# Drives of three states made by ScalarE with time on the partitions, one buffer for the rows of B: a Mamba recurrence on one core

## The chip, the core and the metric

The kernel runs on 1 core of one Trainium2 chip. The time is the device time of one execution in microseconds (us). Lower is better.

## The reference, cut to what matters

The input is x of shape (4, 64, 32, 32). A Mamba block works on two channel orders of each of the 4 images, so on 8 sequences of 1024 steps with 128 inner channels and 16 states. Attention and a chain of small attention and feed-forward steps follow. The change touches the recurrence alone:

```
xc = conv(xi);  u = silu(xc + conv_b)
x_dbl = u @ W_x.T;  dt = softplus(x_dbl[..., :4] @ W_dt.T + b_dt)
Bs, Cs = x_dbl[..., 4:20], x_dbl[..., 20:]
A = -exp(A_log)
# for each step t, channel d, state n:
h[d, n] = exp(dt[t, d] * A[d, n]) * h[d, n] + (dt[t, d] * u[t, d]) * Bs[t, n]
y[t, d] = sum_n h[d, n] * Cs[t, n]
out = ((y + u * D_skip) * silu(z)) @ W_out.T
```

## The kernel before, in words

**Units.** The recurrence is cut into 128 units: `u = 16 * q + n` is state n of sequence q, `NS` is 16. All tiles of a unit have the 128 channels on the partitions and the 1024 time steps along the row. A unit has four parts. The decay `exp(dt * A)` is one ScalarE instruction (`act_exp`, L1324). The drive is `dtu * B`, where `dtu` is dt times u and B's row n is the same on all partitions. The scan (`dve_unit`, L1641) is one VectorE instruction over 1024 steps. The product of the scan's result with C's row (`pool_hc`, L1956) is GpSimd's, and TensorE adds these products of 16 states up in PSUM (`pe_sum`, L816, with the identity as weights, `LAG` = 3 units behind).

**Who makes the drive.** For 10 of 16 states, here called own units, TensorE spreads B's row over the partitions into the PSUM tile `pb[u % 2]` with a selector matrix (`pe_b`, L804, bf16), VectorE multiplies it by `dtu` in place (L1636), and the decay lies in one of three SBUF buffers `da`. For the other six (`POOLED` = 1, 4, 7, 9, 12, 14), a DMA spreads B's row from DRAM scratch into `bb[k % 2]` (`sp_b`, L2127), GpSimd multiplies by `dtu` into `dbu[k % 2]` (`pool_drive`, L1967), and the decay goes into the free `pb[u % 2]`, so that its `act_exp` waits for scan u - 2.

**Order.** Every engine has its own hand-written loop over u. An engine does its instructions in order and waits at semaphores. Beside the units the loops prepare sequence q + 1 at fixed states n:

```
TensorE  n=0: pe_x   n=1: pe_gate(q)  n=3: pe_bc   n=4,6: pe_bc_less  n=7: pe_dt  n=9,10: pe_dt_add
ScalarE  n=1: act_x  n=2: act_gate(q) n=4: act_hi  n=5: act_mid  n=6: act_lo
         n=8,9: act_dt, act_one, act_ln      n=11,12: act_dt_out
VectorE  n=3: dve_y(q-1)                     n=11,12: dve_dtu
```

In iteration u, TensorE does `pe_b(u + 1)` and then `pe_sum(u - 3)`. ScalarE does `act_exp(u + 1)` first, but in iteration n = 1 it does both `act_exp(u + 1)` and `act_exp(u + 2)` ahead of `act_x`, and none at n = 2. GpSimd does `pool_drive(u + 2)` and then `pool_hc(u)`. SyncE does `sp_c(u)`, C's row, and then `sp_b(u + 3)`.

**Three dependences that matter.** `act_x` (SiLU, in another table set, so behind an ACT_TABLE_LOAD) gives u of sequence q + 1. `pe_gate(q)` waits for it, since both use the bank `px[h]`. The sum of state 15 of sequence q - 1 (`pe_sum` at n = 2) stands behind `pe_gate` on TensorE, and `dve_y` at n = 3 waits for that sum. In even sequences `pe_out_late` (L845, n = 14) stands ahead of the next sequence's first `pe_b`.

The two loops around these, as far as they matter here:

```
if u == 0 or n != AHEAD + 1:
    act_exp(act, u + 1)
if n == AHEAD:
    act_exp(act, u + 2)
for h in range(2):
    if q < LAST:
        if n == 1:
            act_x(act, q + 1, h)
```

## Time and profile before

| what | value |
|---|---|
| median of 3 runs | 709.54 us (708.71 to 710.75) |
| the profiled execution, own time | 711.64 us |
| its span, from the first to the last instruction | 709.8 us |
| mean granted TensorE clock | 0.961 |
| first to last scan of the recurrence | 33.2 to 443.7 us of the span |

The profile shows one execution. "Busy" is the time that an engine spent in instructions, idle time is counted before an instruction with the engine or DMA that ended it, and PEld is TensorE's weight load, which runs beside its matmuls. Times in the timeline are from the start of the span.

### The profile page before, as it was taken

The page shows a single profiled execution, that of the slowest core. Times are in us where ns is not written, and L with a number is a line of the kernel's source. Part 1 is how long each engine was busy: PE and PEld are TensorE (multiplying, and loading weights), DVE is VectorE, ACT ScalarE, POOL GpSimd, SP SyncE. Part 2 cuts the span into 40 slices and gives each one's busy share as a digit, 9 for nine tenths or more (in the row PEclk, how much of TensorE's full clock was granted, in tenths as well). Part 3 has the DMA queues.
Part 4 walks back from the last instruction along what each step waited for, and adds up shares of the span by engine and source line. Part 5 has one row for each costly group of instructions (what it writes and reads, how often), then busy time and mean ns, then how long its engine had stood idle before and what let it go on. Part 6 is the DMA issues. An engine that isn't in the chain of part 4 may idle for free.

```text
span 709.8 us, 10911 instructions
## 1 busy us (share of the span) xinstructions
PE 618.5 (87%) x3732; PEld 267.0 (38%) x3732; DVE 581.7 (82%) x622; ACT 415.2 (59%) x643; POOL 451.1 (64%) x240
## 2 busy tenths in 40 slices
PE   8889879889877888988878887988979999999996
PEld 3323222222222212222222222345756446777771
DVE  5799999999999999999999999364365457788755
ACT  4878777668567566766774663353445525544441
POOL 7599999999999999999999999510000220000002
...
GB/s 104 220 267 211 230 227 291 226 259 226 232 232 253 211 250 211 236 217 210 234 233 222 234 241 115 1 1 0 3 5 8 1 20 1 1 2 1 2 2 65
DMA packets 32107, 101.20 MB, mean 143 GB/s; under 512 B 6821, under 2 KB 7342, under 8 KB 32046
## 3 DMA queue, kind: packets, MB, share of 16 engines
...
q10 hardware_dynamic: 1240, 0.88, 0.4%
...
q14 instruction: 28, 0.23, 0.1%
...
## 4 chain that ended last, share of the span: by engine, by line
PE 44%; DVE 23%; issue 19%; ACT 7%; POOL 5%; DMA 1%; DVEq 0%; ACTq 0%; POOLq 0%
DVE hh_all L1641 9%; DVE pb L1636 8%; PE py L279 7%; PE pb L242 6%; PE px L302 5%; PE py L816 5%; POOL hc L1956 4%; PE pb L1044 2%; PE py L1068 2%; PE px L845 2%; PE pb L804 2%; POOL dbu L1967 2%; PE px L292 1%; DVE dtu_all L1615 1%; PE px L763 1%
## 5 line engine op out<-in xcount | busy, mean ns | idle before, releaser
L1956 POOL TENSOR_TENSOR hc<-hh_all,cc 128x1024 f32<-128x1024 f32 x128 | 298.5, 2355 | 6.3 <-DVE hh_all L1641 4.6
L1641 DVE TENSOR_TENSOR_SCAN hh_all<-da,pb 128x1024 f32<-128x1024 f32 x80 | 182.9, 2286 | 3.4 <-ACT da L1324 0.4
L1970 POOL TENSOR_TENSOR yg<-w_xs 128x512 f32<-128x512 f32 x10 | 12.6, 1266 | 227.1 <-DVE w_xs L1783 132.7
L816 PE MATMUL py<-hc,w_cst 64*64 64x512 f32 x1024 | 148.2, 639 | 8.5 <-DVE yg L1652 8.5
L1967 POOL TENSOR_TENSOR dbu<-bb,dtu_all 128x1024 f32<-128x1024 f32 x48 | 113.2, 2358 | 5.0 <-DMA bb<-scr 5.0
L1641 DVE TENSOR_TENSOR_SCAN hh_all<-pb,dbu 128x1024 f32<-128x1024 f32 x48 | 108.9, 2269 | 2.0 <-DVE dtu_all L1615 1.7
L1636 DVE TENSOR_TENSOR pb<-pb,dtu_all 128x1024 f32<-128x1024 f32 x80 | 97.1, 1214 | 3.7 <-PE pb L804 1.2
L804 PE MATMUL pb<-bc,w_sel 128*128 128x512 bf16 x160 | 51.8, 408 | 53.1 <-DVE hh_all L1641 53.0
L1324 ACT ACTIVATE da<-dt_all,w_aneg 128x1024 f32<-128x1024 f32 x80 | 89.8, 1138 | 2.7 <-DVE dt_all L1622 1.8
L1324 ACT ACTIVATE pb<-dt_all,w_aneg 128x1024 f32<-128x1024 f32 x48 | 53.6, 1116 | 64.3 <-DVE hh_all L1641 63.8
L816 PEld LDWEIGHTS py<-hc,w_cst 64*64 64x64 f32 x1024 | 31.2, 136 | 80.9 <-issue 54.4
L804 PEld LDWEIGHTS pb<-bc,w_sel 128*128 128x128 bf16 x160 | 11.0, 99 | 113.4 <-DVE hh_all L1641 83.8
L335 DVE TENSOR_REDUCE gate_all<-pb 128x1 f32<-128x128 f32 (+7 forms) x32 | 22.8, 752 | 19.6 <-PE pb L252 19.5
L279 PE MATMUL py<-w_cst,dbu 128*128 128x128 f32 x208 | 30.3, 286 | 8.1 <-ACT dbu L402 4.8
L402 ACT ACTIVATE bb<-pb,gate_all 128x1024 f32<-128x1024 f32 (+4 forms) x32 | 28.6, 898 | 7.8 <-DVE gate_all L335 7.8
L402 ACT ACTIVATE dbu<-pb,gate_all 128x1024 f32<-128x1024 f32 (+3 forms) x32 | 30.3, 952 | 4.8 <-DVE gate_all L335 4.8
L242 PE MATMUL pb<-w_xs,u_all 64*128 64x512 f32 x128 | 31.8, 615 | 0.0
L410 ACT ACTIVATE da<-py 128x512 f32<-128x512 f32 (+2 forms) x20 | 9.8, 510 | 37.3 <-PE py L279 37.1
L410 ACT ACTIVATE cc<-py 128x512 f32<-128x512 f32 (+1 forms) x20 | 10.7, 553 | 34.6 <-PE py L279 34.6
L355 DVE COPY da<-py 128x512 f32<-128x512 f32 (+2 forms) x28 | 16.1, 610 | 17.6 <-PE py L279 17.6
L279 PE MATMUL py<-w_cst,bb 128*128 128x128 f32 x192 | 27.2, 279 | 3.8 <-ACT bb L402 3.8
L279 PEld LDWEIGHTS py<-w_cst,dbu 128*128 128x128 f32 x208 | 23.2, 144 | 19.1 <-issue 12.4
...
## 6 DMA issues: line engine op xcount, KB each, us to landing
cc<-scr SPq DMA_DIRECT2D x128, 512.0 KB, 4.3
...
```

Of the source, the lines that this page charges most:

```text
L242: part = nc.tensor.matmul(self.s[r][:, o + a:o + a + m], self.qt[rows, g * 128:(g + 1) * 128], self.kt[rows, p * L + a:p * L + a + m], sta ...
L279: last = nc.tensor.transpose(self.pt[:, o + j:o + j + 128], self.p[g % 2][r][:, j:j + 128], self.w["cst"][:, IDN:IDN + 128])
L302: last = nc.tensor.matmul(bank[C * r:C * r + C, 0:128], self.vv[:, p * 8 + j, r, :], self.pts[g % 2][r][:, j * 128:(j + 1) * 128], start=( ...
L335: self.nc.vector.tensor_reduce(self.nm[:, i:i + 1], self.s[r][:, self.start(g):self.start(g) + 128 * self.blocks(g)], AX.X, ALU.max, negat ...
L402: self.nc.scalar.activation(self.p[g % 2][r][:, 0:n], self.s[r][:, self.start(g):self.start(g) + n], ACT.Exp, bias=self.nm[:, i:i + 1], ac ...
L804: last = nc.tensor.matmul(pb[u % 2][:, half(h)], w["sel"][:, n, :], bc3[q % 2][:, half(h)], start=True, stop=True)
L816: last = nc.tensor.matmul(py[part(t), half(r)], ident[part(r), part(r)], hc[u % NHC][part(r), half(t)], start=(n == 0), stop=(n == NS - 1) ...
L1324: nc.scalar.activation(to[:, :], dt[q % 2][:, :], ACT.Exp, scale=w["aneg"][:, n:n + 1]).then_inc(da_done, 1)
L1636: nc.vector.tensor_tensor(pb[u % 2][:, :], pb[u % 2][:, :], dtu[q % 2][:, :], ALU.mult).then_inc(dbu_done, 1)
L1641: nc.vector.tensor_tensor_scan(hh[u % NHH][:, :], decay[:, :], drive[:, :], 0.0, ALU.mult, ALU.add).then_inc(scan_done, 1)
L1956: nc.gpsimd.tensor_tensor(hc[u % NHC][:, :], hh[u % NHH][:, :], cc[u % NCC][:, :], ALU.mult).then_inc(hc_done, 1)
L1967: nc.gpsimd.tensor_tensor(dbu[k % NDB][:, :], bb[k % 2][:, :], dtu[q % 2][:, :], ALU.mult).then_inc(pooled_done, 1)
```

## The change

In sequences 2, 4 and 6 (`FLIPS`) the states are dealt out anew. GpSimd makes the drives of five states (3, 6, 8, 11, 13). States 1, 5 and 15 (`FLIPPED`) are made by ScalarE: with time on the partitions, B of one state is one number per partition, so a drive is eight activations of 128x128 with a scale taken from a column of `b_t` (`act_flip_drive`). Eight TensorE transposes bring it back into `pb` (`pe_b`), and VectorE scans it with no product of its own. The other eight states are own units as before. For this, TensorE transposes B's rows (`pe_flip_b`, n = 7 of the sequence before) and `dtu` (`pe_flip_dtu`, n = 13), and ScalarE copies both to SBUF (`act_flip_b`, `act_flip_dtu`). `pe_dt` of half 1 moves from n = 7 to n = 8 there. The transposed `dtu` lies in `bb[1]`, so the rows of B have `bb[0]` alone in all sequences: `sp_b` waits until GpSimd has made the drive before, and is issued one unit later (u + 2). The two tiles of ScalarE's drives are `ex` and `rl`, which the softplus of the next sequence uses too. `pe_late` moves by one unit.

```diff
-        POOLED = (1, 4, 7, 9, 12, 14)
-        NP = len(POOLED)
+        FLIPS = (2, 4, 6)
+        POOLED = [(3, 6, 8, 11, 13) if q in FLIPS else (1, 4, 7, 9, 12, 14) for q in range(NSEQ)]
+        FLIPPED = [(1, 5, 15) if q in FLIPS else () for q in range(NSEQ)]
...
+        dtu_t, drive_t = bb[1], [ex, rl]
+        b_t = sb("b_t", [128, 128])
...
+        def pe_flip_b(pe, s):
+            pe.wait_ge(px_free[1], freed(s, 1) + 1)
+            pe.wait_ge(bcf_done, 2 * s + 2)
+            for j in range(L // 128):
+                last = nc.tensor.transpose(px[1][:, NS * j:NS * j + NS], bcf[0:NS, j * 128:j * 128 + 128], cst[0:NS, IDN:IDN + NS])
+            last.then_inc(px_full[1], 1)
...
         def pe_b(pe, u):
...
+            if flipped(u):
+                t = flip_count(u)
+                pe.wait_ge(flip_drive, t + 1)
+                for j in range(0, L, 128):
+                    last = nc.tensor.transpose(pb[u % 2][:, j:j + 128], drive_t[t % 2][:, j:j + 128], ident)
+                last.then_inc(b_full, 1)
+                return
...
                         if n == 7:
+                            if h and q + 1 in FLIPS:
+                                pe_flip_b(pe, q + 1)
+                            else:
+                                pe_dt(pe, q + 1, h)
+                        if n == 8 and h and q + 1 in FLIPS:
                             pe_dt(pe, q + 1, h)
+                        if n == 13 and q + 1 in FLIPS:
+                            pe_flip_dtu(pe, q + 1, h)
...
+        def act_flip_b(act, s):
+            act.wait_ge(px_full[1], full(s, BT, 1))
+            atleast(act, flip_drive, flip_count(NS * (s - 1)))
+            nc.scalar.activation(b_t[:, :], px[1][:, 0:128], ACT.Copy).then_inc(flip_in, 1)
...
+        def act_flip_drive(act, u):
...
+            for j in range(L // 128):
+                last = nc.scalar.activation(drive_t[t % 2][:, j * 128:j * 128 + 128], dtu_t[:, j * 128:j * 128 + 128], ACT.Identity,
+                                            scale=b_t[:, NS * j + n:NS * j + n + 1])
+            last.then_inc(flip_drive, 1)
...
+                if n == 7 and q + 1 in FLIPS:
+                    act_flip_b(act, q + 1)
+                act_flip_drive(act, u + 2)
+                if n == 13 and q + 1 in FLIPS:
+                    for h in range(2):
+                        act_flip_dtu(act, q + 1, h)
...
-                nc.vector.tensor_tensor(pb[u % 2][:, :], pb[u % 2][:, :], dtu[q % 2][:, :], ALU.mult).then_inc(dbu_done, 1)
-                dve.wait_ge(dbu_done, k + 1)
+                if not flipped(u):
+                    nc.vector.tensor_tensor(pb[u % 2][:, :], pb[u % 2][:, :], dtu[q % 2][:, :], ALU.mult).then_inc(dbu_done, 1)
+                    dve.wait_ge(dbu_done, product_count(u) + 1)
...
-            atleast(sp, pooled_done, k - 1)
-            sp.dma_start(bb[k % 2][:, :], scr[q % 2, n:n + 1, :].broadcast_to((128, L))).then_inc(bb_in[k % 2], 16)
+            atleast(sp, pooled_done, k)
+            sp.dma_start(bb[0][:, :], scr[q % 2, n:n + 1, :].broadcast_to((128, L))).then_inc(bb_in, 16)
```

**What moves on ScalarE at the start of sequence 2.** From the weight copy that ends sequence 1 (`w_bp`) to the decay of state 4. `da` and `pb` are where a decay goes, `u_all<-px` is `act_x`, `gate_all<-px` is `act_gate`. Before:

```order
L1283 ACTIVATE w_bp<-px,w_vcol 128x1
L1324 ACTIVATE pb<-dt_all,w_aneg 128x1024
L1324 ACTIVATE da<-dt_all,w_aneg 128x1024 x2
L1235 ACT_TABLE_LOAD
L1235 ACTIVATE u_all<-px,w_vcol 128x512 x2
L1305 ACTIVATE gate_all<-px 128x512 x2
L1521 ACT_TABLE_LOAD
```

In the change:

```order
L1336 ACTIVATE w_bp<-px,w_vcol 128x1
L1407 ACTIVATE da<-dt_all,w_aneg 128x1024 x2
L1407 ACTIVATE pb<-dt_all,w_aneg 128x1024
L1285 ACT_TABLE_LOAD
L1285 ACTIVATE u_all<-px,w_vcol 128x512 x2
L1388 ACTIVATE gate_all<-px 128x512 x2
L1610 ACT_TABLE_LOAD
```

The decay into `pb` was that of state 1 and stood first of the three. It is now that of state 3 and stands last of the three, straight ahead of the table load and `act_x`.

**What moves on TensorE in sequence 1, states 7 and 8.** `px<-u_all` is `pe_dt`, one row for each half, and `py<-hc` is `pe_sum`. Before:

```order
L804 MATMUL pb<-bc_1,w_sel 128x512 x2
L816 MATMUL py<-hc,w_cst 64x512 x4
L763 MATMUL px<-u_all,w_wts 128x512 x2
L816 MATMUL py<-hc,w_cst 64x512 x4
```

In the change:

```order
L847 MATMUL pb<-bc_1,w_sel 128x512 x2
L859 MATMUL py<-hc,w_cst 64x512 x4
L785 MATMUL px<-u_all,w_wts 128x512
L792 MATMUL px<-w_cst,bcf 128x16 x8
L859 MATMUL py<-hc,w_cst 64x512 x4
L785 MATMUL px<-u_all,w_wts 128x512
```

The transposes of B (L792) stand behind `pe_dt` of half 0.

**What moves on ScalarE at the same place.** From `act_lo` (`bc_0<-px 32x512`) to the first half's softplus. Before:

```order
L1250 ACTIVATE bc_0<-px 32x512 x2
L1324 ACTIVATE da<-dt_all,w_aneg 128x1024
L1324 ACTIVATE pb<-dt_all,w_aneg 128x1024
L1256 ACTIVATE ex<-px,w_vcol 128x512
```

In the change:

```order
L1300 ACTIVATE bc_0<-px 32x512 x2
L1407 ACTIVATE da<-dt_all,w_aneg 128x1024
L1354 ACTIVATE b_t<-px 128x128
L1407 ACTIVATE pb<-dt_all,w_aneg 128x1024
L1309 ACTIVATE ex<-px,w_vcol 128x512
```

The copy of the transposed B stands between the decays of states 8 and 9, ahead of the softplus.

## Rows read from the trace of the kernel before

**Rows 1.** The page: busy us (share of the span) and instructions of each engine

```profile
PE 618.5 (87%) x3732; PEld 267.0 (38%) x3732; DVE 581.7 (82%) x622; ACT 415.2 (59%) x643; POOL 451.1 (64%) x240
```

**Rows 2.** Windows, mid recurrence: length, busy PE, PEld, DVE, ACT, POOL, clock, DMA, GB/s

```profile
160.00:210.00 50.00, 42.55 (x227) 12.53 (x225) 48.68 (x30) 34.48 (x44) 50.00 (x23) 1.00 0.66 232
```

**Rows 3.** The page's costliest groups: busy us, mean ns | idle before, releaser

```profile
L1956 POOL TENSOR_TENSOR hc<-hh_all,cc 128x1024 f32<-128x1024 f32 x128 | 298.5, 2355 | 6.3 <-DVE hh_all L1641 4.6
L1967 POOL TENSOR_TENSOR dbu<-bb,dtu_all 128x1024 f32<-128x1024 f32 x48 | 113.2, 2358 | 5.0 <-DMA bb<-scr 5.0
L1636 DVE TENSOR_TENSOR pb<-pb,dtu_all 128x1024 f32<-128x1024 f32 x80 | 97.1, 1214 | 3.7 <-PE pb L804 1.2
```

**Rows 4.** Waits of VectorE, 55 to 445 us: total us, times, longest

```profile
DVE pb L1636 <- PE pb L804: 1.2, 2, 0.9
```

**Rows 5.** Timeline, VectorE, sequence 1, states 9 to 11: start us, us

```profile
112.39 2.26 DVE L1641 TENSOR_TENSOR_SCAN hh_all<-pb,dbu 128x1024 f32<-128x1024 f32 x1
...
115.81 2.29 DVE L1641 TENSOR_TENSOR_SCAN hh_all<-da,pb 128x1024 f32<-128x1024 f32 x1
...
119.25 2.29 DVE L1641 TENSOR_TENSOR_SCAN hh_all<-da,pb 128x1024 f32<-128x1024 f32 x1
```

**Rows 6.** Timeline, ScalarE, sequence 1: decay 9, softplus, decay 11

```profile
109.06 1.12 ACT L1324 ACTIVATE pb<-dt_all,w_aneg 128x1024 f32<-128x1024 f32 x1 [1.92 <-DVE hh_all L1641]
110.21 0.69 ACT L1256 ACTIVATE ex<-px,w_vcol 128x512 f32<-128x512 f32 x1
110.79 0.68 ACT L1257 ACTIVATE rl<-px,w_vcol 128x512 f32<-128x512 f32 x1
...
117.59 1.14 ACT L1324 ACTIVATE da<-dt_all,w_aneg 128x1024 f32<-128x1024 f32 x1
```

**Rows 7.** Timeline, TensorE, sequence 1, state 7

```profile
106.90 0.61 PE L804 MATMUL pb<-bc,w_sel 128*128 128x512 bf16 x2 [2.20 <-DVE hh_all L1641]
...
108.46 1.98 PE L763 MATMUL px<-u_all,w_wts 128*128 128x512 f32 x4
```

**Rows 8.** The page: groups of 128x128 transposes in the attention, with their weight loads

```profile
L279 PE MATMUL py<-w_cst,dbu 128*128 128x128 f32 x208 | 30.3, 286 | 8.1 <-ACT dbu L402 4.8
...
L279 PEld LDWEIGHTS py<-w_cst,dbu 128*128 128x128 f32 x208 | 23.2, 144 | 19.1 <-issue 12.4
```

**Rows 9.** Timeline, ScalarE, start of sequence 4

```profile
239.87 1.28 ACT L1235 ACT_TABLE_LOAD   x1
241.16 1.26 ACT L1235 ACTIVATE u_all<-px,w_vcol 128x512 f32<-128x512 f32 x2
...
245.69 1.12 ACT L1324 ACTIVATE pb<-dt_all,w_aneg 128x1024 f32<-128x1024 f32 x1 [0.19 <-DVE hh_all L1641]
```

**Rows 10.** Timeline, TensorE, start of sequence 4: gate, B of state 3, sum 15

```profile
241.90 1.65 PE L793 MATMUL px<-w_xs,w_wts 64*64 64x512 f32 x8 [0.17 <-ACT u_all L1235]
243.49 0.61 PE L804 MATMUL pb<-bc,w_sel 128*128 128x512 bf16 x2
244.02 1.09 PE L816 MATMUL py<-hc,w_cst 64*64 64x512 f32 x8
```

**Rows 11.** Timeline, VectorE, start of sequence 4: the two halves of y

```profile
245.57 1.26 DVE L1652 TENSOR_TENSOR yg<-py,gate_all 128x512 f32<-128x512 f32 x2
```

**Rows 12.** Timeline, TensorE and VectorE, end of sequence 4

```profile
281.84 0.61 PE L804 MATMUL pb<-bc,w_sel 128*128 128x512 bf16 x2 [1.62 <-DVE hh_all L1641]
...
286.83 0.60 PE L804 MATMUL pb<-bc,w_sel 128*128 128x512 bf16 x2
...
287.54 1.23 DVE L1636 TENSOR_TENSOR pb<-pb,dtu_all 128x1024 f32<-128x1024 f32 x1
```

**Rows 13.** Landings of `bb` (60 to 440 us), then one of `cc` at 191 us; GpSimd's timeline

```profile
DMA to landing us min/median/max: 4.6/5.0/7.8
...
DMA to landing us min/median/max: 3.4/3.4/3.4
...
207.12 4.65 POOL L1956 TENSOR_TENSOR hc<-hh_all,cc 128x1024 f32<-128x1024 f32 x2
```

More of the change, by code:

```diff
@@ L502, in pooled, with flipped, flip_count, product_count @@
         def pooled(u):
-            return u % NS in POOLED
+            return u % NS in POOLED[u // NS]
+        def flipped(u):
+            return u % NS in FLIPPED[u // NS]
         def pool_count(u):
-            return NP * (u // NS) + sum(1 for n in POOLED if n < u % NS)
+            return sum(1 for v in range(u) if pooled(v))
+        def flip_count(u):
+            return sum(1 for v in range(u) if flipped(v))
+        def product_count(u):
+            return own_count(u) - flip_count(u)
         def own_count(u):
@@ L764, in pe_dt, with pe_flip_dtu @@
                              skip_group_check=True).then_inc(px_full[h], 1)
+        def pe_flip_b(pe, s):
[4 more added lines that the diff above has]
+            last.then_inc(px_full[1], 1)
+        def pe_flip_dtu(pe, s, h):
+            pe.wait_ge(px_free[h], freed(s, h) + 2 + h)
+            pe.wait_ge(dtu_done, 2 * s + h + 1)
+            for j in range(0, HALF, 128):
+                last = nc.tensor.transpose(px[h][:, j:j + 128], dtu[s % 2][:, h * HALF + j:h * HALF + j + 128], ident)
+            last.then_inc(px_full[h], 1)
         def pe_dt_add(pe, s, h):
@@ L1230, in act_x @@
         def act_x(act, s, h):
-            act.wait_ge(px_full[h], full(s, X))
+            act.wait_ge(px_full[h], full(s, X, h))
             if s >= 2:
@@ L1254, in act_dt @@
         def act_dt(act, s, h):
-            act.wait_ge(px_full[h], full(s, DT))
+            act.wait_ge(px_full[h], full(s, DT, h))
+            if s - 1 in FLIPS:
+                used = max(n for n in FLIPPED[s - 1] if n < 9)
+                act.wait_ge(b_full, own_count(NS * (s - 1) + used) + 1)
             nc.scalar.activation(ex[:, half(h)], px[h][:, :], ACT.Abs, bias=w["bdt"][:, :])
@@ L2153, in _ @@
             sp_scratch(sp, 0)
-            for u in range(3):
+            for u in range(2):
                 sp_b(sp, u)
```

101 lines of the change are left out of this document (63 added, 38 removed).

## The prediction

> **What bounds the kernel now.** I read the page's busy line first [rows 1]: no engine is full over the whole span, so it decides nothing, and the stage must be looked at by itself. The windows of the recurrence do that [rows 2]: in 50 us GpSimd is busy for 50.0, VectorE for 48.7, and ScalarE for 34.5. Two engines are full there. The groups give their work [rows 3]: GpSimd has 22 products of 2.36 us a sequence, some 51 us (a little less, since neighbours overlap), and VectorE has 16 scans, ten products of 1.21 us and small work, also some 51 us. The waits say that neither has slack: VectorE waits for its products' input only twice, 1.2 us in all [rows 4], and GpSimd waits 4.6 us for scans in the whole recurrence [rows 3]. So a microsecond comes off only if it comes off both, and a wait on either costs its full length. That is how each edit is priced: on VectorE's path, with GpSimd's looked at for what it supplies.
>
> **What is removed.** In each of sequences 2, 4 and 6 VectorE makes 8 products where it made 10. A product takes 1.21 us [rows 3], with the step to the next instruction 1.23. From scan to scan with a product it is 119.25 - 115.81 = 3.44 [rows 5], so 2.21 without. Two in three sequences: 6 x 1.23 = **-7.4**. GpSimd has one product less in each, 3 x 2.32 = 7.0 (half of the 4.65 for two [rows 13]). Both full engines get about the same relief, so it could all count, and this is the most that the change can bring. What ScalarE and TensorE are given lies beside that, unless one of their results is late. I went through each for what stands behind it.
>
> **Preparing B, sequences 1, 3 and 5.** ScalarE's copy of transposed B stands ahead of the decay of state 9. TensorE can start on it only when it has done B's row of state 8 (106.90, released by scan 6), a sum, and `pe_dt` of half 0, which starts at 108.46 and takes half of 1.98 [rows 7], so at 109.45. Eight transposes of 16 rows are not in the trace; full ones are, at 23.2 / 208 = 0.11 us for each weight load [rows 8], so I take 0.9, which gives 110.35, and 0.15 for the copy. ScalarE starts decay 9 at 110.5 and not at 109.06 [rows 6]: **1.45 later**. From there to decay 11 it works without a gap: softplus from 110.21, decay 11 from 117.59 to 118.73 [rows 6]. VectorE starts scan 11 at 119.25 [rows 5], so it has 0.5 to spare. It waits 1.45 - 0.5 = 0.95. Three times: **+2.9**. Bounds: nothing, if ScalarE's copy comes 1 us earlier than I think, and 2 us each, where TensorE is granted the lower clock at that moment. The shift of `pe_dt` of half 1 costs nothing: it is needed 4 us after decay 9.
>
> **The start of sequences 2, 4 and 6.** This is the place I trust least and that weighs most. The decay of state 3 goes into `pb`, waits for scan 1, and stands directly ahead of the table load and `act_x`. Before, these three decays were done before scan 1 had ended, and the load came at 239.87 [rows 9]. Now the chain runs from the end of scan 1: the decay 1.12 and 0.05 to start (the latter an estimate), the load 0.02 + 1.29 (239.87 to 241.16), the gate's matmuls 0.74 after the first SiLU started, 1.6 for them (241.90 to 243.49), and the first half of the sum of state 15, 0.55 of 1.09 [rows 9, 10]. That is 5.4 us to the first half of y. VectorE in the same time does the product and scan of state 2, 1.23 + 2.2 = 3.45, and then wants y. Before, the sum ended at 245.1 and y started at 245.57 [rows 10, 11], straight behind the scan. So each of the three now waits 5.4 - 3.45 = 1.9: **+5.7**. Lower end 1.3 each, the gate at its shortest; upper end 2.4, if the sum's second half is what y waits for.
>
> At this load a page speaks against the change. The row shows a load that starts as the decay ends and is over in 1.29 us, with the SiLU right behind it [rows 9]; my chain goes by that. The Trainium skill (ScalarE: Activation LUTs, What ACT_TABLE_LOAD costs) gives 1283 ns for the load and some 1380 ns for a drain at each switch. It is a rival below.
>
> The transposes of the first flipped drive also stand ahead of `pe_x` on TensorE, and they wait for scan 15 of the sequence before. They make the product of state 2 up to 0.8 late. That lies inside the wait for y and costs nothing as long as that wait is there.
>
> **ScalarE's drives.** Eight activations of 128 columns with a scale from SBUF. Two of 512 columns with such an operand start 0.58 apart; between 0.69 for 512 and 1.14 for 1024 a column costs 0.88 ns, so for 128 I take 0.58 - 0.34 = 0.24, and with the last one's end 2.1 us for a drive [rows 6]. The ends are 1.2, half of it, and 3. State 1's is made in the idle end of the sequence before, and state 15's behind decay 14 with some 3 us to spare. State 5's falls behind decay 4. By the chain above it and decay 5 are done 1 us before scan 5 wants them, because VectorE has waited for y. Nothing for the three.
>
> **The end of sequences 2, 4 and 6.** TensorE goes from scan 13 to B's row of the next sequence without a gap: 281.84 to 287.43, and VectorE's product starts at 287.54, right behind [rows 12]. Eight transposes at 30.3 / 208 = 0.146 [rows 8] take 1.2 to 1.3 in place of 0.6: 0.65 later, less the 0.1 of slack. **+0.5** each, 1.5 in all. The ends are 0 and 1.5 each (at 0.27 a transpose, the duration of a lone one).
>
> **One buffer for B.** A row is now fetched only when GpSimd's drive before it is done. Where pooled states are 2 apart (two such pairs a sequence, 16 in all), two products of C, 4.65 us, lie between. `bb` landed after 4.6 to 7.8, median 5.0, but it always followed a `cc` by 0.4 us; a transfer of the same size with nothing ahead landed after 3.4 [rows 13]. Now C's row of that unit was issued two products earlier and B's row goes first. I take 4 us, so it is hidden under those products; in some it will not be: **+0.3**. The ends are 0 and 16 x 0.45 = 7. Behind this wait on SyncE's queue C's next row is held by one GpSimd product, 2.3 us; it is wanted four such products later.
>
> **The sum.** -7.4 + 2.9 + 5.7 + 1.5 + 0.3 = **+3.0 us**. For the profiled execution that is 711.64 + 3.0 = 714.6. That execution was 2.1 above the median of the runs, which is what I forecast: 709.54 + 3.0 = 712.5 us.
>
> **Rivals.**
> - *The waits for y do not come, and the relief arrives.* The place is state 3 of sequences 2, 4, 6; the point is whether the chain from scan 1 to y is under 3.5 us. For it: ScalarE has 15 of 50 us free [rows 2], and the relief is equal on both full engines. Against it: each link of the chain is a row. -7.4 + 2.9 + 1.5 + 0.3 = -2.7: 706.8. If the preparation is hidden too, 704. Chance 0.18.
> - *The wait for y stands and the two others are hidden*, as the order of the two small waits depends on tenths of a microsecond: -7.4 + 5.7 + 0.3 + 1 = -0.4: 709.1. Chance 0.22.
> - *The single buffer is late.* If B's row lands after 5.0 as before, every near pair costs 0.4: +6.4, part of it inside other waits, so 3.0 + 4 = 7: 716.5. For it: the median. Against it: the order on the queue. Chance 0.12.
> - *The switch of tables waits for ScalarE to run empty when it follows directly on a decay.* The place is the load behind the decay of state 3. If that costs as long as the load itself again, 1.29 [rows 9], the chain to y grows by so much in three sequences: 3.0 + 3.9 = 6.9: 716.4. No wait stands behind the load in the row, so 0.05. By the figure of the page named above this would be 3 x 1.38 = 4.1 instead, an estimate.
>
> **How the numbers follow.** About 0.3%, 2.1 us, is what a measurement of this kernel can tell from no change: under 707.4 is faster, over 711.7 slower. The forecast itself has 0.43, nearly all above 711.7. Slower gets 0.58, with the third and fourth rival; within 0.3%, 0.23, which is the second rival and the edge of the forecast; faster 0.19. The range goes from the first rival to beyond the third: 706.5 to 717.5. The bounds of the terms alone would reach from 705 to over 720.
>
> **What would show it.** Right: in sequences 2, 4 and 6 VectorE sits idle for some 2 us ahead of y, released by TensorE's sum (L859) or shows it as a wait for `py`; a wait of about 1 us at scan 11 of sequences 1, 3 and 5, released by ScalarE's decay; 0.5 at the first product of sequences 3, 5 and 7, released by TensorE. GpSimd waits for `bb` under 1 us in all. Wrong: if VectorE has no wait at y, the second largest term is gone and the kernel is faster. If GpSimd waits for `bb` at most near pairs, the buffer term was too small. If the flipped scans (states 1, 5, 15) wait for `pb`, I had ScalarE's drives or their transposes too short.

## The result and the profile after

| | before | the change |
|---|---|---|
| median in one job (4 runs each) | 710.14 us | 721.77 us (719.73 to 724.35) |
| ratio | | 1.0181, 95% interval 1.0155 to 1.0206 |
| profiled execution, own time | 711.64 us | 721.56 us |
| its span, mean granted TensorE clock | 709.8 us, 0.961 | 719.8 us, 0.962 |
| end of the last scan of the recurrence | 443.7 us | 458.1 us |

The change is slower by 1.8%, some 12 to 13 us, where 3 were forecast. In the profiled execution the recurrence ends 14.4 us later. What follows it, code that the change does not touch, took 261.7 us there and 266.1 before. In a later run it took 260.2, so that part scatters between executions, and I compare by sequence below.

First the page of the change: busy time of the engines, then the groups that answer to [rows 3].

```profile
PE 627.3 (87%) x3840; PEld 276.7 (38%) x3840; DVE 575.6 (80%) x616; ACT 440.1 (61%) x724; POOL 445.5 (62%) x237
...
L2046 POOL TENSOR_TENSOR hc<-hh_all,cc 128x1024 f32<-128x1024 f32 x128 | 299.6, 2359 | 24.1 <-PE py L859 12.7
L2057 POOL TENSOR_TENSOR dbu<-bb,dtu_all 128x1024 f32<-128x1024 f32 x45 | 106.1, 2358 | 7.3 <-DMA bb<-scr 7.3
...
L1726 DVE TENSOR_TENSOR pb<-pb,dtu_all 128x1024 f32<-128x1024 f32 x74 | 89.9, 1215 | 12.7 <-PE pb L847 10.5
```

These are lines of the whole page; `py` is TensorE's sum, `hc` GpSimd's product with C. The work went as announced: 74 products on VectorE, 45 drives on GpSimd. But GpSimd idles 24.1 us ahead of its products of C, 12.7 of them for TensorE's sums. VectorE's waits in the recurrence (33 to 456 us; total, times, longest) are the view that answers to [rows 4]:

```profile
DVE pb L1726 <- PE pb L847: 10.5, 9, 4.3
DVE hh_all L1731 <- POOL dbu L2057: 4.9, 5, 3.4
DVE hh_all L1731 <- ACT pb L1407: 2.4, 4, 1.0
...
DVE hh_all L1731 <- ACT da L1407: 1.9, 5, 0.4
DVE yg L1742 <- PE py L859: 1.8, 2, 1.0
```

The wait for y, my largest cost, is 1.8 in all. Ten microseconds go to B's rows from TensorE and five to GpSimd's drives. I had nothing of that size for either. To see where, take the start of the first scan of each sequence from the timeline and subtract it from the next one's (us):

| sequence | 0 | 1 | 2 | 3 | 4 | 5 | 6 |
|---|---|---|---|---|---|---|---|
| before | 52.0 | 50.5 | 51.1 | 50.9 | 51.1 | 52.4 | 50.7 |
| the change | 52.1 | 55.1 | 56.0 | 53.4 | 51.7 | 53.5 | 51.7 |
| forecast difference | 0 | +0.95 | -0.1 | +0.95 | -0.1 | +0.95 | -0.1 |
| measured difference | 0 | +4.6 | +4.9 | +2.5 | +0.6 | +1.1 | +1.0 |

(The forecast for sequences 2, 4 and 6 is -2.46 + 1.9 + 0.5; the 0.3 for the buffer is spread over all.) Two thirds of the loss lie in sequences 1 and 2. How much such a value scatters is shown by sequence 0, where only the buffer of B differs: over all profiles of this study it took 51.5 to 53.7. A difference of 1 in one profile means little. Sequence 2 moves more than that with TensorE's clock (below), so a wait with its releaser says more than a length.

**Sequence 1: SyncE's queue.** Timeline of SyncE's issues before (first fence) and in the change (second): `w_xs<-w_xm` are the spreads of the inputs of sequences 4, 5 and 6, each a pair of transfers of 256 KB, of which the first is shown.

```profile
100.66 0.47 SPq L2148 DMA_DIRECT2D w_xs<-w_xm  x1
...
104.15 0.47 SPq L2148 DMA_DIRECT2D w_xs<-w_xm  x1
...
108.06 0.43 SPq L2127 DMA_DIRECT2D bb<-scr  x1
108.61 0.47 SPq L2148 DMA_DIRECT2D w_xs<-w_xm  x1
```

```profile
105.27 0.32 SPq L2216 DMA_DIRECT2D bb<-scr  x1
105.68 0.47 SPq L2237 DMA_DIRECT2D w_xs<-w_xm  x1
...
109.16 0.47 SPq L2237 DMA_DIRECT2D w_xs<-w_xm  x1
...
111.20 1.45 SPq L2237 DMA_DIRECT2D w_xs<-w_xm  x1
...
114.38 0.81 SPq L2216 DMA_DIRECT2D bb<-scr  x1
```

With one buffer the `bb` of 105.27 had to wait for GpSimd's drive before it. The three pairs of spreads stood behind it, so they started 5.0, 5.0 and 2.6 us later and closer together, ahead of the `bb` of state 12, which was issued at 114.38 and not at 108.06. The four `cc` issued between 110 and 118 us landed after 9.1 to 10.0 us (the median over the kernel is 4.5), that of 110.32 at 119.38. Then, on GpSimd and VectorE:

```profile
119.50 2.36 POOL L2046 TENSOR_TENSOR hc<-hh_all,cc 128x1024 f32<-128x1024 f32 x1 [2.38 <-issue]
...
120.14 2.29 DVE L1731 TENSOR_TENSOR_SCAN hh_all<-da,pb 128x1024 f32<-128x1024 f32 x1 [0.41 <-ACT da L1407]
...
124.02 2.35 POOL L2057 TENSOR_TENSOR dbu<-bb,dtu_all 128x1024 f32<-128x1024 f32 x1 [2.15 <-DMA bb<-scr]
...
126.40 2.29 DVE L1731 TENSOR_TENSOR_SCAN hh_all<-pb,dbu 128x1024 f32<-128x1024 f32 x1 [3.40 <-POOL dbu L2057]
```

GpSimd stops for 2.38 us, until that row of C has landed, and for 2.15 until the row of B has, and scan 12 waits 3.40. Scan 11 starts at 120.14 against 119.25 [rows 5], so the preparation of B costs 0.89 here; I had said 0.95.

**The start of sequence 2: a chain of three engines.** Timeline of TensorE, ScalarE and VectorE in the change:

```profile
135.91 0.87 PE L963 MATMUL px<-w_cst,w_xs 128*128 128x128 f32 x5
136.60 0.28 ACT L1328 ACTIVATE w_xs<-px 128x128 f32<-128x128 f32 x1 [2.65 <-PE px L963]
...
138.88 2.44 ACT L1377 ACTIVATE ex<-bb,b_t 128x128 f32<-128x128 f32 x8
...
141.47 1.06 PE L843 MATMUL pb<-w_cst,ex 128*128 128x128 f32 x8 [2.71 <-ACT ex L1377]
...
143.91 2.07 PE L754 MATMUL px<-w_xs,w_wts 128*128 128x512 f32 x2
...
148.67 0.59 PE L847 MATMUL pb<-bc,w_sel 128*128 128x512 bf16 x2
...
149.31 1.23 DVE L1726 TENSOR_TENSOR pb<-pb,dtu_all 128x1024 f32<-128x1024 f32 x1 [4.25 <-PE pb L847]
```

The late weights are turned (L963), ScalarE copies them and a decay, makes the first flipped drive until 141.32, TensorE transposes it, and only then comes `pe_x` with B's row of state 2 behind it. The product of state 2 waits 4.25 us. The first two pairs of `pe_x` took 2.07 and 1.34 us where later ones take 1.02, which is TensorE at the lower of its two clocks (1.2 GHz against 2.4) for part of the way: the granted clock was 0.65 in 132 to 138 us and, behind the idle 2.71 us of the row at 141.47, 0.80 in 144 to 150. At the end of the sequence the clock fell again: the first product of sequence 3 waited 2.41 us for its row of B. These waits account for the length: 51.1 before, less 2.46 for the two products, plus 4.25, 2.41, 0.50 for a drive of GpSimd and 0.24 for a decay, is 56.0.

### The profile page after: what moved, and what is told of

Read it like the earlier page. It is cut to its first block, busy times and chain, and to the rows that moved or that the text cites. A ratio compares the mean times of both kernels' runs of the same rounds, so it can differ in the third digit from the quotient of the medians.

```text
span 719.8 us, 11232 instructions
## 1 busy us (share of the span) xinstructions
PE 627.3 (87%) x3840; PEld 276.7 (38%) x3840; DVE 575.6 (80%) x616; ACT 440.1 (61%) x724; POOL 445.5 (62%) x237
## 4 chain that ended last, share of the span: by engine, by line
PE 46%; DVE 19%; issue 15%; ACT 13%; POOL 3%; DMA 2%; DVEq 0%; SPq 0%; ACTq 0%; POOLq 0%
DVE hh_all L1731 8%; PE py L279 7%; PE pb L242 6%; PE py L859 5%; PE px L302 5%; DVE pb L1726 5%; ACT da L1407 2%; PE pb L1087 2%; POOL hc L2046 2%; PE py L1111 2%; PE px L888 2%; PE pb L847 2%; POOL dbu L2057 1%; PE px L292 1%; PE px L754 1%
## 5 line engine op out<-in xcount | busy, mean ns | idle before, releaser
L2046 POOL TENSOR_TENSOR hc<-hh_all,cc 128x1024 f32<-128x1024 f32 x128 | 299.6, 2359 | 24.1 <-PE py L859 12.7
L1731 DVE TENSOR_TENSOR_SCAN hh_all<-da,pb 128x1024 f32<-128x1024 f32 x83 | 188.9, 2284 | 6.1 <-DVE pb L1726 1.9
L859 PE MATMUL py<-hc,w_cst 64*64 64x512 f32 x1024 | 152.0, 649 | 9.7 <-DVE yg L1742 6.1
L2060 POOL TENSOR_TENSOR yg<-w_xs 128x512 f32<-128x512 f32 x10 | 12.7, 1270 | 222.4 <-DVE w_xs L1873 132.7
L2057 POOL TENSOR_TENSOR dbu<-bb,dtu_all 128x1024 f32<-128x1024 f32 x45 | 106.1, 2358 | 7.3 <-DMA bb<-scr 7.3
L1731 DVE TENSOR_TENSOR_SCAN hh_all<-pb,dbu 128x1024 f32<-128x1024 f32 x45 | 102.4, 2276 | 8.9 <-POOL dbu L2057 4.9
L1726 DVE TENSOR_TENSOR pb<-pb,dtu_all 128x1024 f32<-128x1024 f32 x74 | 89.9, 1215 | 12.7 <-PE pb L847 10.5
L1407 ACT ACTIVATE da<-dt_all,w_aneg 128x1024 f32<-128x1024 f32 x83 | 93.6, 1141 | 6.5 <-DVE hh_all L1731 3.6
L847 PE MATMUL pb<-bc,w_sel 128*128 128x512 bf16 x148 | 47.6, 405 | 41.0 <-DVE hh_all L1731 40.9
L1407 ACT ACTIVATE pb<-dt_all,w_aneg 128x1024 f32<-128x1024 f32 x45 | 50.1, 1114 | 43.2 <-DVE hh_all L1731 42.0
```

What stands on the lines that cost most here:

```text
L847: last = nc.tensor.matmul(pb[u % 2][:, half(h)], w["sel"][:, n, :], bc3[q % 2][:, half(h)], start=True, stop=True)
L859: last = nc.tensor.matmul(py[part(t), half(r)], ident[part(r), part(r)], hc[u % NHC][part(r), half(t)], start=(n == 0), stop=(n == NS - 1) ...
L1407: nc.scalar.activation(to[:, :], dt[q % 2][:, :], ACT.Exp, scale=w["aneg"][:, n:n + 1]).then_inc(da_done, 1)
L1726: nc.vector.tensor_tensor(pb[u % 2][:, :], pb[u % 2][:, :], dtu[q % 2][:, :], ALU.mult).then_inc(dbu_done, 1)
L1731: nc.vector.tensor_tensor_scan(hh[u % NHH][:, :], decay[:, :], drive[:, :], 0.0, ALU.mult, ALU.add).then_inc(scan_done, 1)
L2046: nc.gpsimd.tensor_tensor(hc[u % NHC][:, :], hh[u % NHH][:, :], cc[u % NCC][:, :], ALU.mult).then_inc(hc_done, 1)
```

## The experiments

All times of a sequence are read as above, from one profile each. "The change" below is the kernel after. The kernel before was run in each job (medians 709.3, 708.2, 709.4 and 709.9 us) and the ratios are to it; they are not exactly the quotients of the medians. e7_spread and all runs from e10_best on have the spreads apart.

| run | median us | ratio, 95% interval | seq. 1 | 2 | 3 | 4 | 5 | 6 |
|---|---|---|---|---|---|---|---|---|
| e1_single | 713.95 | 1.0066 (1.0038 to 1.0095) | 54.8 | 51.6 | 52.4 | 50.8 | 50.9 | 50.8 |
| e2_slots | 720.33 | 1.0149 (1.0104 to 1.0194) | 53.1 | 55.1 | 53.6 | 53.3 | 53.3 | 51.7 |
| e3_late | 724.6 | 1.0217 (1.0147 to 1.0287) | 53.4 | 52.4 | 53.6 | 51.7 | 53.8 | 51.7 |
| e4_swap | 722.58 | 1.0177 (1.0130 to 1.0224) | 53.6 | 54.2 | 53.6 | 52.8 | 53.5 | 53.3 |
| e7_spread | 721.52 | 1.0128 (1.0047 to 1.0208) | 52.9 | 51.8 | 53.5 | 51.7 | 53.5 | 53.3 |
| e8_two | 720.48 | 1.0136 (1.0077 to 1.0196) | 54.0 | 51.6 | 54.6 | 53.4 | 53.5 | 51.7 |
| e9_xfirst | 724.28 | 1.0255 (1.0171 to 1.0338) | 55.6 | 56.6 | 53.5 | 51.9 | 53.5 | 52.1 |
| e10_best | 716.8 | 1.0107 (1.0080 to 1.0134) | 51.1 | 52.2 | 54.6 | 53.5 | 53.5 | 52.0 |
| e11_endb | 715.51 | 1.0087 (1.0052 to 1.0122) | 51.7 | 53.1 | 51.5 | 51.7 | 51.3 | 53.4 |
| e12_one3 | 719.2 | 1.0106 (1.0055 to 1.0157) | 53.1 | 54.8 | 53.5 | 52.7 | 53.5 | 52.8 |
| e13_all2 | 709.5 | 0.9993 (0.9974 to 1.0013) | 50.9 | 51.4 | 52.5 | 52.8 | 51.4 | 51.1 |
| e14_all3 | 712.69 | 1.0024 (0.9996 to 1.0052) | 51.0 | 53.5 | 51.5 | 51.1 | 51.5 | 51.1 |
| e15_sum2 | 707.8 | 0.9969 (0.9946 to 0.9993) | 50.5 | 51.1 | 50.9 | 49.7 | 51.5 | 51.3 |
| e16_sum3 | 707.15 | 0.9955 (0.9926 to 0.9984) | 50.5 | 50.4 | 51.5 | 50.2 | 51.4 | 51.4 |

### The single buffer alone, and two buffers where they fit

```diff
-        FLIPS = (2, 4, 6)
+        FLIPS = ()
```

> The change without flipped sequences: the deal of states of the kernel before in all sequences, but one buffer for the rows of B, fetched two units ahead. Queue theory: SyncE waits for the buffer ahead of the spreads of xs in sequence 1, the next row of B then lands late behind them; GpSimd and VectorE lose 4 to 5 us in sequence 1 and under 1 us in all other sequences together: 714 to 716 us. Near-pair theory (the row always comes too late where two pooled states are 2 apart): 0.4 us at each of 16 pairs, in every sequence: 716 to 718 us, and sequence 1 no worse than the others. If neither buffer cost is real: 710 us.

The run also keeps the later issue of B's rows (u + 2) and `pe_late` one unit later. 1.0066, and +4.3 us in sequence 1. Sequence 3 is 1.5 longer, 5 is 1.5 shorter, the others of the table within 0.5. VectorE's waits:

```profile
DVE hh_all L1731 <- POOL dbu L2057: 3.9, 2, 3.5
```

Both waits, 3.5 and 0.35 us, are in sequence 1; the near pairs of the other sequences show none. The queue theory holds and the near-pair theory falls.

```diff
-            sp.dma_start(bb[0][:, :], ...
+            sp.dma_start(bb[slot(u)][:, :], ...
```

(`slot(u)` alternates between both buffers outside the flipped sequences and is 0 inside; the row is then issued at u + 3 again, and ScalarE's copy of the transposed `dtu` waits for one drive of GpSimd more.)

> The change with two buffers for the rows of B wherever the second does not hold the transposed dtu (sequences 0, 1, 3, 5, 7, the last pooled state of each in the first buffer), fetched three units ahead there. Queue theory: sequence 1 falls from 55.1 to some 51.5 us, nothing else changes: 721.8 - 3.5 = 718 us. If the 55.1 come from the copy of B on ScalarE instead: under 1 us is gained.

The waits for GpSimd's drives and for `bb` in sequence 1 are gone, but it falls by 2.0 and no more. The preparation of B, 0.89 in the change, now makes VectorE wait 0.94, 0.83, 0.28 and 0.41 us. TensorE's clock made the difference:

```profile
107.82 1.01 PE L853 MATMUL pb<-bc,w_sel 128*128 128x512 bf16 x2 [3.01 <-DVE hh_all L1738]
```

The same row of B took 0.60 us in the change, after 2.19 us of idle, and the granted clock in 108 to 112 us was 0.59 here and 1.00 there. Sequence 2 hardly changed, and the whole came out 1.4 us under the change and not 3.5.

### The turn of B elsewhere

```diff
-                if n == 7 and q + 1 in FLIPS:
+                if n == 8 and q + 1 in FLIPS:
                     act_flip_b(act, q + 1)
```

> The change with ScalarE's copy of the transposed B behind the softplus of half 0 (state 8) and not ahead of the decay of state 9. Theory of the copy's wait: the waits of VectorE at states 9 to 11 of sequences 1, 3 and 5 go (0.9, 2.5 and 2.5 us in the trace): 721.8 - 5 = 717 us, less in sequence 1, where the buffer's wait lies behind it. Rival, the lower TensorE clock at state 8 alone makes them late: 721 us.

The decay was free, but the bank of `px` was not: `pe_dt` of half 1 waits for the copy to have read it, and B's row of state 10 stands behind that on TensorE. Sequence 3, timeline of e3_late:

```profile
222.37 1.10 PE L785 MATMUL px<-u_all,w_wts 128*128 128x512 f32 x2 [2.06 <-ACTq L1356]
...
223.94 1.23 DVE L1726 TENSOR_TENSOR pb<-pb,dtu_all 128x1024 f32<-128x1024 f32 x1 [1.52 <-PE pb L847]
```

The expectation failed: sequences 3 and 5 stayed at 53.6 and 53.8, with a wait for TensorE in place of one for ScalarE. So later (with the spreads apart, as in e7_spread below) both were moved to state 13, behind the last use of that bank:

```diff
-                if n == 7 and q + 1 in FLIPS:
-                    act_flip_b(act, q + 1)
                 act_flip_drive(act, u + 2)
                 if n == 13 and q + 1 in FLIPS:
+                    act_flip_b(act, q + 1)
```

(and `pe_flip_b` at n = 13 ahead of `pe_flip_dtu`, with the order of pieces to match)

> With the spreads of xs apart (as in the run before), B's rows are turned and copied at state 13 of the sequence ahead, just ahead of the turned dtu, and no longer at state 7 ahead of decay 9. My theory: the turn of B costs about 2.4 us of a sequence where it stands now, because ScalarE's decays 9 to 11 stand behind the copy, which waits for TensorE; at state 13 ScalarE has time. Sequences 1, 3 and 5 fall to 51.5, 51.5 and 52.4 (52.9, 53.5 and 53.5 with the spreads apart alone), the others as there (51.7, 51.7, 52.5 +-0.8); whole 716.0. Rival: the copy and the eight transposes now lengthen the chain to the drive of state 1 at the start of the flipped sequence, which is waited for by pe_x and the product of state 2: sequences 2, 4 and 6 rise by as much, 53 or more, whole 719 to 721.

Sequences 1, 3 and 5: 51.7, 51.5, 51.3. That is 1.2 to 2.1 less than in e7_spread, as expected or better. What ScalarE waited for ahead of the three copies shows it, first in the change, where it stood idle for 12.3 us with the decays behind, then in e11_endb:

```profile
PE px L792: 12.3, 3
```

```profile
L1351 ACT ACTIVATE b_t<-px 128x128 f32<-128x128 f32 x3 | 0.8, 278 | 0.7 <-PE px L792 0.7
```

Sequences 2 and 6 rose by 1.3 and 0.1. That of sequence 2 is the rival's direction, though within the scatter.

### The spreads apart

```diff
-                if NS + 8 <= u < NS + 11:
-                    spread(u - NS - 4)
+                if u in (NS + 5, NS + 9, 2 * NS):
+                    spread({NS + 5: 4, NS + 9: 5, 2 * NS: 6}[u])
```

> SyncE issues the spreads of xs of sequences 4, 5 and 6 at iterations 5 and 9 of sequence 1 and 0 of sequence 2 (the change: 8, 9 and 10 of sequence 1, in a row); the rest is the change as it is. My theory of sequence 1 is that the issue queue is in order: the bb of state 9 waits there for GpSimd's drive of state 7, behind it stand the three spreads (256 KB each, twice 128 KB), and behind those the rows that GpSimd needs in states 12 and 14. If so, sequence 1 falls from 55.1 us to 53.0 (+-0.7: what the turn of B costs there stays, as it did with two buffers), VectorE's wait of 3.4 us for GpSimd's drive of state 12 is gone, sequences 2 to 7 stay as in the change, and the whole is 719.5. Rival: the transfers of bb and cc are late by themselves (the sixteen DMA engines are loaded by the 512 KB rows), the place of the spreads matters little: sequence 1 stays above 54.5 and the wait for dbu stays above 2.

(A spread is twice 256 KB, not twice 128.) Sequence 1 took 52.9 (expected 53.0), and its long wait for GpSimd's drive of state 12 is gone. That wait alone does not prove the queue: in e4_swap below, where SyncE's order is that of the change, it is 0.30, since the preparation had made VectorE itself late. GpSimd shows it better. In e4_swap it stops twice at this place, 1.91 and 1.78 us, for rows that landed after 8.1 to 8.6 us; here it does not stop there, and these rows landed after 4.2 to 7.8. So the queue is the cause, and two buffers are not needed to cure it. The cure is not complete: with a spread moved ahead of it, the row of state 7 landed after 6.0 us, and scan 9 waits 1.24 us for GpSimd's drive; the row of B of state 8 took 1.03 us here as well.

Not expected was sequence 2, 51.8 in place of 56.0. The product of state 2 now waits 2.00 us instead of 4.25, and the one at the end 0.77 instead of 2.41:

```profile
145.83 1.23 DVE L1726 TENSOR_TENSOR pb<-pb,dtu_all 128x1024 f32<-128x1024 f32 x1 [2.00 <-PE pb L847]
```

Windows of the same stretch (length, busy PE, PEld, DVE, ACT, POOL, granted clock, DMA share, GB/s), the change first, then e7_spread:

```profile
132.00:138.00 6.00, 5.01 (x26) 1.44 (x25) 5.60 (x4) 3.11 (x9) 6.00 (x4) 0.65 0.43 162
138.00:144.00 6.00, 3.29 (x25) 1.68 (x21) 5.72 (x4) 5.71 (x13) 4.57 (x2) 0.92 0.83 279
144.00:150.00 6.00, 6.00 (x18) 2.39 (x22) 1.75 (x2) 3.77 (x4) 4.65 (x2) 0.80 0.47 180
```

```profile
133.00:139.00 6.00, 4.05 (x29) 1.59 (x27) 5.96 (x4) 4.20 (x14) 5.91 (x4) 1.00 0.97 217
139.00:145.00 6.00, 5.36 (x24) 2.59 (x25) 4.80 (x3) 4.01 (x7) 4.69 (x3) 1.00 0.78 303
145.00:151.00 6.00, 5.75 (x35) 1.64 (x35) 5.14 (x5) 5.36 (x7) 5.25 (x3) 1.00 0.59 199
```

The same chain at the full clock costs half. The spreads are not what sets that clock: e2_slots, without the late rows, was granted 0.53 in 133 to 139 us and took 55.1, and e3_late, with SyncE's order of the change, was granted 1.00 in 134 to 146, waited 2.01 at this product and took 52.4. So some 4 of the 4.9 us that sequence 2 lost in the profile of the change come and go with TensorE's clock. The four times of this run scattered from 715 to 726, and its median is that of the change; what it shows lies in the profile.

### Which of the flipped sequences costs, and what stands ahead of `pe_x`

```diff
-        FLIPS = (2, 4, 6)
+        FLIPS = (4, 6)
```

> Only sequences 4 and 6 are changed (the list of flipped sequences is 4, 6); sequence 2 runs as before, the single buffer stays everywhere. My theory says that sequence 2 is the dearest of the three, since there the turned late weights, their copies on ScalarE and the first flipped drive stand in a chain ahead of pe_x: sequence 2 falls from 56.0 to 51.5 (what the single buffer alone gave), sequence 1 stays at 54.8 (the queue of SyncE, as with the single buffer alone), sequences 3 to 6 stay as in the change (53.4, 51.7, 53.5, 51.7); whole 717.0. Rival: the loss comes equally from each flipped sequence (about 4 us each), then the whole is about 717.5 too but with sequence 2 not below 53 and sequences 4 and 6 higher; the split by sequence tells them apart.

Sequence 2 at 51.6, as expected: its loss is its own. Sequences 3 and 4 came out 1.2 and 1.7 above the change, so the whole gained less than I expected. In sequence 4 it is the product at the end, which waited 2.48 us (0.78 in the change).

```diff
+                if n == 0 and q in FLIPS and q < LAST:
+                    for h in range(2):
+                        pe_x(pe, q + 1, h)
                 pe_b(pe, u + 1)
```

> In flipped sequences TensorE issues pe_x of the next sequence ahead of the four transposes of the first flipped drive (state 1), so pe_x no longer waits for ScalarE's drive. My theory: the 4.25 us that VectorE waited for the product of state 2 in sequence 2 fall to under 2 and the y waits of sequences 4 and 6 (0.8 + 0.8) to under 0.8 together; sequence 2 falls from 56.0 to 53.5, sequences 4 and 6 by 0.5 to 1 each; whole 718.0. Rival: the wait changes its place, for now the transposes of state 1 stand behind pe_x (3.6 us at the lower granted clock), VectorE waits for them before scan 1 and nothing is won: sequences 2, 4 and 6 within 0.7 of the change, whole 721 to 723.

The rival: the wait only changed its place, and in sequence 2 it even grew. In sequences 4 and 6 the product no longer waits, but y does, 1.74 us each (0.79 and 0.99 in the change).

```profile
140.98 2.04 PE L754 MATMUL px<-w_xs,w_wts 128*128 128x512 f32 x2 [2.33 <-ACT w_bp L1339]
...
147.05 2.29 DVE L1734 TENSOR_TENSOR_SCAN hh_all<-da,pb 128x1024 f32<-128x1024 f32 x1 [4.79 <-PE pb L843]
```

The first row also says what else `pe_x` waits for in sequence 2: ScalarE's copy of the late weights (`w_bp`), from the same bank.

The other way is to change who makes which drive. e4_swap gives state 4 and not 3 to GpSimd, so that no decay into `pb` stands ahead of the table load:

```diff
-        POOLED = [(3, 6, 8, 11, 13) if q in FLIPS ...
+        POOLED = [(4, 6, 8, 11, 13) if q in FLIPS ...
```

> The change with state 4 instead of state 3 made by GpSimd in sequences 2, 4 and 6, so that no decay that waits for scan 1 stands ahead of the table load. Theory of the chain to y: act_x runs ahead again, y starts right behind scan 2, 1.6 us are gained in each of sequences 4 and 6 and up to 2 in sequence 2: 721.8 - 4 = 718 us. Rival: the first flipped drive's transposes ahead of pe_x keep the product of state 2 late (0.8 of the 1.6 stay), and GpSimd has two pairs 2 apart back to back: 720 us.

The wait for y is gone, and no time with it. The near pairs 4, 6, 8 make GpSimd's drives late: in the three flipped sequences VectorE waits for those six times, 5.6 us in all (1.2 in the change). It was the rival's case, and the whole is above both figures.

e12_one3 exchanges states 1 and 3, on top of the spreads apart:

```diff
-        POOLED = [(3, 6, 8, 11, 13) if q in FLIPS ...
-        FLIPPED = [(1, 5, 15) if q in FLIPS ...
+        POOLED = [(1, 6, 8, 11, 13) if q in FLIPS ...
+        FLIPPED = [(3, 5, 15) if q in FLIPS ...
```

> With the spreads of xs apart, in flipped sequences GpSimd makes the drive of state 1 as before and ScalarE that of state 3 (the change: 3 and 1). So the first flipped transposes come behind pe_x, and pe_x waits for nothing of ScalarE's. My theory: the waits at the start of the flipped sequences (product of state 2 and y) go, and the two VectorE products that each flipped sequence has less come out: sequences 2, 4 and 6 at 50.0 (+-0.7) each, instead of 51.7; whole 714.5. Rival: ScalarE's drive of state 3 now stands between act_x and the gate and ahead of the next decays (2.4 us), and VectorE waits for those or for the drive of state 3 itself: sequences 2, 4 and 6 stay at 51.3 or more, whole 718 or more, with waits for PE pb L843 or ACT da in the trace.

The numbers are the rival's, the place is neither's. Sequences 2, 4 and 6 took 54.8, 52.7 and 52.8. VectorE waits for y, three times, 6.5 us in all: the sum of state 15 stands on TensorE behind the transposes of state 3, which wait for ScalarE's drive. That is what the last two runs took up.

### All together

> Four edits together: only sequences 4 and 6 flipped, two buffers for B's rows outside the flipped sequences, the spreads of xs apart from each other, pe_x ahead of the first flipped transposes. By my sum of the parts: sequence 1 50.7, sequence 2 51.2, sequence 3 53.0 (the turn of B), sequence 4 51.2, sequence 5 53.0, sequence 6 51.2: about 4.5 over the kernel before, 714.0. If also the turn of B costs nothing once the queue is free, 709 to 710; under 708 would be a version that beats both. Rival: the parts hide each other, and what remains is GpSimd, whose drives come later in flipped sequences: 716 or more with waits for dbu above 3 us in all.

(Sequences 4 and 6 alone, two buffers, spreads apart, `pe_x` first, each edit as above.) Sequence 1 was right and 3 and 4 were 1.6 and 2.3 above; 716.8 in place of 714, the rival's figure with another mechanism: no wait for `dbu` above 0.5, but 5.3 us for y in three waits of the recurrence. The longest, 3.25 at the start of sequence 4, is the chain of my forecast at the lower clock: the decay of state 3, the load, the SiLU, then the gate's matmuls and the sum, 3.7 us for both, where the change took 2.5. TensorE had stood idle for 2.96 us ahead of them.

> All edits that took a wait away, in sequences 4 and 6 only: spreads apart, two buffers for B's rows outside the flipped sequences, B turned at state 13, state 1 on GpSimd and state 3 on ScalarE. By the sum of the parts, with what the kernel before shows in brackets: sequence 1 50.7 (50.5), 2 51.2 (51.1), 3 51.5 (50.9), 4 49.8 (51.1), 5 52.0 (52.4), 6 49.8 (50.7): 1.7 under the kernel before, 707.5. If this holds, the idea was worth its 1.2 us per product, and its cost lay in what stood in line behind it. Rival: ScalarE and TensorE have no such slack, each step taken from VectorE comes back as a wait for them: 711 or more.

> As the run before it, with all three flipped sequences (2, 4 and 6). Sequence 1 51.2, sequence 2 49.8, the rest as there: 706.5. Rival: in sequence 1 and at the start of 2 the turned late weights (five transposes, their copies, two more matmuls) share ScalarE and TensorE with the turn of B and of dtu; then sequence 1 or 2 is over 52 and the run is slower than its neighbour with two flipped sequences, 709 or more.

(Both without `pe_x` first; B turned at state 13, states 1 and 3 exchanged.) e13_all2 is level with the kernel before, 0.9993, and e14_all3 is 1.0024 (its sequence 2, 53.5, is what its rival named): nearly all of the loss of 1.8% is gone by changing places, with as many drives on ScalarE in e14_all3. The gain is not there. Start of sequence 6 in e13_all2:

```profile
352.98 1.06 PE L849 MATMUL pb<-w_cst,rl 128*128 128x128 f32 x8 [1.34 <-ACT rl L1381]
...
353.97 1.09 PE L865 MATMUL py<-hc,w_cst 64*64 64x512 f32 x8
355.09 1.29 DVE L1745 TENSOR_TENSOR yg<-py,gate_all 128x512 f32<-128x512 f32 x2 [1.36 <-PE py L865]
...
355.29 2.37 POOL L2049 TENSOR_TENSOR hc<-hh_all,cc 128x1024 f32<-128x1024 f32 x1 [1.37 <-PE py L865]
```

One set of transposes holds the sum (L865), and the sum holds both full engines for 1.4 us. So:

```diff
+                early = u + 1 < UNITS and flipped(u + 1)
+                if early:
+                    pe_sum(pe, u - LAG)
                 pe_b(pe, u + 1)
-                pe_sum(pe, u - LAG)
+                if not early:
+                    pe_sum(pe, u - LAG)
```

> As e13_all2 (two flipped sequences), and TensorE makes the sum of the state three back ahead of the transposes of a flipped drive instead of behind them. Theory: sum 15 stood behind the transposes of state 3, which waited 1.3 us for ScalarE's drive, and y behind both; now y starts straight behind scan 2, sequences 4 and 6 fall by 1.4 each to 49.8 (GpSimd's own 21 products of 2.36 are 49.6, which no edit here goes under), the whole is 2.5 under the kernel before, 707. Rival: the transposes then come 1.1 us later, scan 3 waits for them instead, GpSimd gets its scans no earlier, sequences 4 and 6 stay at 51.1 and the whole within 0.3% of the kernel before.

> As e14_all3 (three flipped sequences) with the same edit. Theory: sequences 2, 4 and 6 at 51.5 (the end of 2 and TensorE's lower granted clock keep it above the others), 49.8 and 49.8, whole 708 to 709. Rival as for the run before it: no change against e14_all3.

Both beat the kernel before: 0.9969 (0.9946 to 0.9993) and 0.9955 (0.9926 to 0.9984). The gain is small beside what a measurement can tell, but both intervals lie below 1. What the last edit alone did is clear for three flipped sequences, where the intervals with and without it do not meet, and not for two, where they overlap. At the start of sequence 6 in e15_sum2 y follows scan 2 without a wait, and the transposes still come in time for scan 3:

```profile
344.47 2.29 DVE L1738 TENSOR_TENSOR_SCAN hh_all<-da,pb 128x1024 f32<-128x1024 f32 x1
...
345.99 1.07 PE L849 MATMUL pb<-w_cst,rl 128*128 128x128 f32 x8 [0.48 <-ACT rl L1385]
346.67 1.26 DVE L1749 TENSOR_TENSOR yg<-py,gate_all 128x512 f32<-128x512 f32 x2
...
347.86 2.28 DVE L1738 TENSOR_TENSOR_SCAN hh_all<-da,pb 128x1024 f32<-128x1024 f32 x1
```

Windows of its sequences 4 and 6:

```profile
237.66:287.35 49.69, 44.60 (x246) 15.11 (x244) 47.63 (x28) 40.92 (x68) 49.46 (x22) 1.00 0.68 228
338.84:390.17 51.33, 45.55 (x244) 15.04 (x242) 47.74 (x28) 40.91 (x68) 49.85 (x23) 0.97 0.69 229
```

Sequence 4 took 49.69 (expected 49.8), 1.4 less than before, though two products of VectorE are 2.46. GpSimd is busy for 49.46 of the stretch, but it is not the floor that I took it for: two of its products in a row take 4.65, so 21 are 48.8, and from the product of state 0 to that of the next sequence it took 48.9. The rest stands on VectorE's side as two waits, 0.49 us for a drive of GpSimd and 0.77 for the product at the end. Sequence 6 came to 51.3, since the product at its end waited 1.9 us for TensorE (granted clock 0.97 over the sequence). e16_sum3's sequences 2, 4 and 6 took 50.4, 50.2 and 51.4 (expected 51.5, 49.8 and 49.8). The profiled recurrences themselves end only 0.9 and 0.4 us earlier than before (442.8 and 443.3); the gain rests on 12 and 11 runs.

## Why the prediction was wrong in size

**One buffer: the step that failed first.** "The buffer term +0.3" was worked out at the near pairs of pooled states, where it was right, since nothing waited there. The sentence behind it looked only at C's next row on SyncE's queue. What stands on that queue in sequence 1, the three spreads, was not gone through. e1_single puts it at +4.3 us there, and e7_spread takes it away with the single buffer kept. The rival of a late buffer had the right size (716.5 by 4 us) by luck, at places that did not wait. Over the recurrence VectorE waited 4.9 us for GpSimd's drives where the term had 0.3.

**"It lies inside the wait for y and costs nothing": the step that failed second.** In sequence 4 it holds: the product of state 2 waits 0.84 us (I had written up to 0.8) and y 0.79, together 1.63 against the 1.9 forecast. In sequence 2 the same transposes have the late weights ahead of them, which I had seen move by one unit and not priced; the product waits 4.25 us, and y then not at all. At the full clock the product waited 2.00 (e7_spread), so the 1.9 would have come out there, by luck, at another place. What the term lacked is the clock: every matmul in it was taken at the full one, and at the lower one the start of sequence 2 cost 2.3 us more.

**Preparing B** was right where TensorE ran at the full clock (0.89 against 0.95) and took 2.5 of sequence 3, over the upper bound, "2 us each", that I had named and not weighted. In sequence 5 it was the same: waits of 0.97, 0.82, 0.28 and 0.41 us, at a granted clock of 0.71 in 325 to 329. The difference of 1.1 in the table looks like the forecast only because the kernel before had itself waited 1.24 us there. The row of B ahead of it took 1.03 us and not 0.59:

```profile
218.33 1.03 PE L847 MATMUL pb<-bc,w_sel 128*128 128x512 bf16 x2 [3.01 <-DVE hh_all L1731]
...
223.09 0.28 ACT L1354 ACTIVATE b_t<-px 128x128 f32<-128x128 f32 x1 [4.52 <-PE px L792]
```

TensorE had stood idle for 3.01 us before that row. With the turn at state 13 the term is nearly gone (e11_endb).

**The end of the flipped sequences** made the next product wait 0.78 and 0.77 in sequences 4 and 6 (0.5 forecast) and more in sequence 2, where the product waited 2.41 us after a row of B at the lower clock.

**ScalarE's drives** took 2.43 us each, where 2.1 was forecast, and the eight transposes 1.06 to 1.15, where I had 1.2 to 1.3. The Trainium skill (TensorE: Matmul & The Clock Gate, Part 4: PE-mode transpose) has some 275 ns for a transpose in a kernel; the record of one is 0.27 us here too (median of 72), so the page agrees, but eight in a row overlap and take 0.13 to 0.14 us each. No flipped scan waited for its transposes; "Nothing for the three" held outside the start of the sequences.

**The products removed, -7.4.** This term held. Sequence 4 of the change is 51.1 - 2.46 plus its waits, 0.84, 0.79, 0.78, 0.33 and 0.29, which is 51.7, as measured. The products came off in full; the new waits outweighed them.

**The rival of the table switch** fell. In sequence 4 of the change the load follows directly on the decay:

```profile
254.11 1.12 ACT L1407 ACTIVATE pb<-dt_all,w_aneg 128x1024 f32<-128x1024 f32 x1 [4.47 <-DVE hh_all L1731]
...
255.25 1.28 ACT L1285 ACT_TABLE_LOAD   x1
...
256.54 1.26 ACT L1285 ACTIVATE u_all<-px,w_vcol 128x512 f32<-128x512 f32 x2
```

It starts 0.02 us after the decay has ended, and the SiLU 0.01 after the load. The load of 1283 ns in the Trainium skill (ScalarE: Activation LUTs, What ACT_TABLE_LOAD costs) agrees; the drain of 1380 ns beside it does not show.

What stays open: why TensorE is granted the lower clock in some executions at the turn from sequence 1 to 2 and not in others (0.65 in the change, 1.00 in e7_spread and e3_late, 0.53 in e2_slots), and with that some 4 us of sequence 2. Also not tried: putting `pe_out_late` behind B's row at the end of the flipped sequences.
